# Softplus of the Mamba step in four VectorE instructions, with new orders of issue

## The reference

```python
xdbc = xi @ Wx
dt_in = xdbc[..., :DT_RANK]                       # 8 columns
dt = jax.nn.softplus(dt_in @ Wdt + bdt)           # 256 channels, bdt in -4 .. -2
def step(h, inp):                                 # over the 512 tokens
    dA = jnp.exp(dt_t[:, :, None] * A)
    h = dA * h + (dt_t * u_t)[:, :, None] * B_t[:, None, :]
    y = jnp.einsum('bds,bs->bd', h, C_t)
```

## Time and profile before

| | |
|---|---|
| median of 3 runs | 2081.15 us (2073.28 to 2085.22) |
| the profiled execution's own time | 2084.03 us |
| its span | 2081.9 us, 27272 instructions |
| busy | PE 1770.7 (85%), DVE 1582.0 (76%), ACT 1093.9 (53%), POOL 798.9 (38%) |
| mean granted TensorE clock | 0.919 |
| chain that ended last | PE 49%, DVE 18%, issue 14%, ACT 8%, POOL 5%, DMA 2% |
| ScalarE table loads | 196, 1283 ns each |

### The profile page before, as it was taken

One profiled execution on the slowest core, in us unless ns is written; L12 is line 12 of the kernel. 1 busy time (PEld: TensorE's weight loads), 2 busy tenths in 40 slices (PEclk: granted clock), 3 DMA queues, 4 the chain that ended last, 5 costly groups with the idle time before them and its releaser, 6 DMA issues.

```text
span 2081.9 us, 27272 instructions
## 1 busy us (share of the span) xinstructions
PE 1770.7 (85%) x8504; PEld 818.7 (39%) x8544; DVE 1582.0 (76%) x2148; ACT 1093.9 (53%) x1494; POOL 798.9 (38%) x632
## 2 busy tenths in 40 slices
PE   4543488989988999989998999989998999989888
PEld 1220133443343434443343434443444435434545
DVE  1888888779886898879986898869987899641404
ACT  2424376357734775357734676367734675334122
POOL 0345544244543454234543445235533446220101
PEclk9665698999999999999999999999999999999989
DMA  7889998458845786458745786558745786400000
GB/s 211 223 208 222 225 218 206 112 147 193 195 105 147 168 203 167 119 136 196 194 106 144 168 204 165 123 137 194 194 116 136 167 204 184 107 11 0 6 1 5
DMA packets 108200, 310.54 MB, mean 149 GB/s; under 512 B 16000, under 2 KB 32272, under 8 KB 108048
## 3 DMA queue, kind: packets, MB, share of 16 engines
q1 hardware_dynamic: 93840, 280.36, 56.1%
q10 hardware_dynamic: 14208, 28.32, 4.2%
HBM read 288.71 MB, written 19.92 MB: 148 GB/s over the span
## 4 chain that ended last, share of the span: by engine, by line
PE 49%; DVE 18%; issue 14%; ACT 8%; POOL 5%; DMA 2%; DVEq 1%; ACTq 0%; POOLq 0%
PE ps_pair L700 11%; PE ps_pair L856 8%; PE ps_pair L797 8%; DVE sb_hst L1278 6%; PE ps_pair L785 6%; PE ps_pair L650 4%; PE ps_pair L876 3%; POOL sb_hc L1540 3%; ACT sb_mix L1100 2%; PE ps_y L632 2%; DMA sb_ring<-spread_dram 2%; DVE ps_in L1270 2%; DVE sb_dd L1256 2%; DVE sb_dd L1252 2%; PE ps_pair L800 2%
## 5 line engine op out<-in xcount | busy, mean ns | idle before, releaser
L1540 POOL TENSOR_TENSOR sb_hc<-sb_hst,sb_crep 128x512 f32<-128x512 f32 x512 | 658.8, 1296 | 891.4 <-DVE sb_hst L1278 566.0
L1278 DVE TENSOR_TENSOR_SCAN sb_hst<-sb_ring,ps_in 128x512 f32<-128x512 f32 x512 | 621.4, 1214 | 74.6 <-POOL sb_hc L1540 50.6
L952 ACT ACTIVATE sb_ring<-sb_ring,sb_A 128x512 f32<-128x512 f32 x512 | 344.1, 712 | 163.3 <-DMA sb_ring<-spread_dram 105.3
L1270 DVE TENSOR_TENSOR ps_in<-sb_ring,ps_brow 128x512 f32<-128x512 f32 x512 | 354.6, 693 | 21.5 <-DMA sb_ring<-spread_dram 4.1
L856 PE MATMUL ps_pair<-sb_mix,sb_ew 128*128 128x512 f32 x512 | 270.6, 668 | 6.1 <-DVE sb_g L1357 3.3
L921 ACT ACT_TABLE_LOAD x196 | 251.5, 1283 | 14.3 <-DVE sb_xd L1318 5.6
L632 PE MATMUL ps_y<-sb_hc,sb_const 128*32 128x512 f32 x1024 | 153.1, 673 | 70.7 <-POOL sb_hc L1540 58.4
L797 PE MATMUL ps_pair<-sb_g,sb_h 128*128 128x512 f32 x320 | 161.4, 627 | 26.8 <-ACT sb_mix L1100 12.0
L785 PE MATMUL ps_pair<-sb_h,sb_g 128*128 128x512 f32 (+3 forms) x512 | 164.6, 453 | 5.1 <-DVE sb_nmax L1409 4.3
L856 PEld LDWEIGHTS ps_pair<-sb_mix,sb_ew 128*128 128x128 f32 x512 | 103.0, 212 | 154.9 <-issue 115.0
L876 PEld LDWEIGHTS ps_pair<-sb_ew,sb_eh 128*128 128x128 f32 x1024 | 120.0, 192 | 23.3 <-issue 22.5
(11 more groups left out here) (218 smaller groups left out, 2147.0 us busy)
## 6 DMA issues: line engine op xcount, KB each, us to landing
sb_ring<-spread_dram SPq DMA_DIRECT2D x512, 512.0 KB, 5.7
spread_dram<-sb_dd ACTq DMA_DIRECT2D x32, 512.0 KB, 2.9
sb_brep<-cut_dram ACTq DMA_DIRECT2D x16, 256.0 KB, 3.7
sb_crep<-cut_dram ACTq DMA_DIRECT2D x16, 256.0 KB, 4.0
sb_xtok<-in_L_attn_x_dram SPq DMA_DIRECT2D x8, 256.0 KB, 5.0
sb_ew<-in_L_ffn_w_dram SPq DMA_DIRECT2D x2, 1024.0 KB, 8.4
out_dram<-sb_yy ACTq DMA_DIRECT2D x8, 256.0 KB, 2.3
sb_h<-in_L_ffn_h_w_dram SPq DMA_DIRECT2D x1, 1024.0 KB, 7.3
```

Source lines behind the costliest of these rows:

```text
L952: act.activation(ring[:, n % RING, 0, :], ring[:, n % RING, 0, :], ACT.Exp, scale=A[d][:, g:g + 1]).then_inc(sem["dA"], 1)
L1270: dve.tensor_tensor(ps_in[n % 2][:], ring[:, n % RING, 1, :], ps_brow[:], ALU.mult).then_inc(sem["dbu"], 1)
L1278: dve.tensor_tensor_scan(hst[:, HST_SLOT[n], :], ring[:, n % RING, 0, :], ps_in[n % 2][:], 0.0, ALU.mult, ALU.add).then_inc(sem["scan"], 1)
L1540: pool.tensor_tensor(hc[:, n % 6, :], hst[:, HST_SLOT[n], :], crep[n // NU][:], ALU.mult).then_inc(sem["hc"], 1)
```

## The change

The bias becomes a row of the dt product: sb_wdt has 41 rows per direction (8 weights, 32 zeros, the bias), sb_xd a row of ones behind B and C. ScalarE's Identity becomes Square(t / sqrt(3) - 0.75 / sqrt(3)), to which 0.8125 is added, the same polynomial; GpSimd's product is gone; the mask is made by ScalarE as Relu(0.008 - t) in a tile of its own (sb_tsel), where a bit pattern other than zero counts as true. VectorE then has four instructions (and the memset of one column as before): series, masked copy, max(v, 0) plus logarithm out of PSUM in one, times u. The bank of a dtp product is released by dt, not by the early maximum. The first loads wait for GpSimd's memset of sb_wdt. A half takes two steps of the head stream where it took three, GpSimd has no head stream, and all order strings are written anew.

```diff
 def freed_head(name):
     if name[:3] == "dtp":
-        return "rpos", int(name[3]) + 1
+        return "dt", int(name[3]) + 1
 ...
 ORDER = dict(
     PE=(
-        "xxxxxxuxxxxrxruxrxrxruxrurxrhrurhhhrxhrhuhrrurxhhhxurruxhhxrrhurhhhxhxurhxxrhrhurhrrrrrrrrrrrrrrrurrrrxxhrrrrr"
+        "xxxxxxuxrxxruxrxhrurxhrurxuhxxrrhrrxhrrrurhhhuxrrrurxurhxxuxhrhxxrrxxhrrrurxrrrrrrrrrrrrhrhhuhrurhurrxrrrrrrru"
 ...
             with nc.allow_non_contiguous_dma(reason="per-channel vectors, once"):
+                sp.wait_ge(w_zero, 1)
 ...
-                rows = slice(64 * d, 64 * d + R)
+                rows = slice(64 * d, 64 * d + R + 2 * S + 1)
 ...
             def dt_step(row, hf, made):                      # ScalarE
-                act.wait_ge(sem["dt"], row("dt", hf))
+                act.wait_ge(sem["du"], row("du", hf))
                 act.wait_ge(sem["kept"], row("kept", 16 * hf))
-                act.activation(dd[:, 0, :], made()[:], ACT.Abs, bias=cols[d][:, 1, h:h + 1]
-                               ).then_inc(sem["absd"], 1)
+                act.activation(dd[:, 0, :], made()[:], ACT.Abs).then_inc(sem["absd"], 1)
 ...
-                act.activation(tser, texp[:], ACT.Identity, scale=1.0 / 3.0, bias=mhalf[:, 0:1]
+                act.activation(tser, texp[:], ACT.Square, scale=THIRD, bias=vertex[:, 0:1]
                                ).then_inc(sem["third"], 1)
+                act.activation(tsel[:], texp[:], ACT.Relu, scale=-1.0, bias=small[:, 0:1]).then_inc(sem["small"], 1)
                 act.activation(dd[:, 0, :], texp[:], ACT.Ln, bias=one[:, 0:1]).then_inc(sem["logd"], 1)
 ...
-            def dt_step(row, hf, k, made):                   # VectorE
-                if k == 0:
-                    dve.wait_ge(sem["absd"], row("absd", hf + 1))
-                    dve.tensor_scalar(tpos[:], made[:], cols[d][:, 1, h:h + 1], 0.0,
-                                      ALU.add, ALU.max).then_inc(sem["rpos"], 1)
-                elif k == 1:
-                    dve.wait_ge(sem["series"], row("series", hf + 1))
-                    link(1, dve.scalar_tensor_tensor(tser, tser, 1.0, texp[:], ALU.add, ALU.mult))
-                    dve.wait_ge(sem["logd"], row("logd", hf + 1))
-                    link(2, dve.tensor_scalar(tsel, texp[:], SMALL, None, ALU.is_le))
-                    dve.memset(tick[:], 0.0)
-                    link(3, dve.copy_predicated(dd[:, 0, :], tsel, tser))
-                    dve.tensor_tensor(dd[:, 0, :], dd[:, 0, :], tpos[:], ALU.add).then_inc(sem["dt"], 1)
+            def dt_step(row, hf, made):
+                dve.wait_ge(sem["third"], row("third", hf + 1))
+                dve.scalar_tensor_tensor(tser, tser, 0.8125, texp[:], ALU.add, ALU.mult).then_inc(sem["series"], 1)
+                dve.wait_ge(sem["series"], row("series", hf + 1))
+                dve.wait_ge(sem["small"], row("small", hf + 1))
+                dve.wait_ge(sem["logd"], row("logd", hf + 1))
+                dve.memset(tick[:], 0.0)
+                dve.copy_predicated(dd[:, 0, :], tsel[:].bitcast(U32), tser).then_inc(sem["log1p"], 1)
+                dve.wait_ge(sem["log1p"], row("log1p", hf + 1))
+                dve.scalar_tensor_tensor(dd[:, 0, :], made[:], 0.0, dd[:, 0, :], ALU.max, ALU.add).then_inc(sem["dt"], 1)
                 dve.wait_ge(sem["dt"], row("dt", hf + 1))
                 dve.tensor_tensor(dd[:, 1, :], dd[:, 0, :], u[d][:, h, :], ALU.mult).then_inc(sem["du"], 1)
 ...
-            def dt_step(row, hf):                            # GpSimd
-                pool.wait_ge(sem["third"], row("third", hf + 1))
-                pool.tensor_tensor(tser, tser, texp[:], ALU.mult).then_inc(sem["series"], 1)
```

101 lines of the change are left out of this document (44 added, 57 removed).

## The result

The changed kernel takes 2058.86 us in the median of four runs (2051.44 to 2060.53), the kernel before, run beside it, 2082.07. The ratio is 0.9888 with a 95% interval of 0.985 to 0.9927: 1.1% faster. The forecast was 2048 with a range of 2018 to 2092, so the time lies in the range and 11 us above the forecast. The sum behind the forecast did worse than that: its main term, 25 us from the five passes of the loop, came to 3.7.

The account below looks back on a forecast made before the run. TensorE, busy 92% of a pass, was taken to set the time, with VectorE's softplus making it wait. Six items sum to -5.0 us a pass; -37 in all from 2084, 2.9 to the median, 4 put back: 2048, range 2018 to 2092.

Parts of the forecast that it names:

- VectorE's saving: Softplus on VectorE: three instructions out, one in of 0.744 us; saves 2.05 us a half, 8.2 us a pass.
- Item 1: TensorE's pause before dtp3 goes, as VectorE starts half 2's series earlier; gain 3.66 + 3.4 = 7.1 us a pass.
- item 2: TensorE's pause before the query product goes, as half 0's softplus leaves xn's way; gain 3.40 + 3.3 = 6.7 us a pass.
- the prediction's own sign: TensorE's pauses before dtp3 and the query product: the forecast is wrong if they come back at other products.
- Item 3: x0 moves behind the last score, where TensorE had waited for the split (1.04 us); gain 1.9 us a pass.
- Item 4: dtp3's bank held until dt: second h2 product waits about 1 us, the norm's chain costs 1; loss 2 a pass.
- Item 5: One more unit (0.69 + 1.21 us) among the score maxima, where VectorE has no slack; loss 2 us a pass.
- Item 6: dtp1 between second and third block of exponentials: 3.3 us waiting plus a slow stretch of 3.4; loss 6.7 a pass.
- B: ScalarE takes VectorE's place: Relu and table loads, 5.2 us mid-pass, eat the gain; 2081, chance 0.18 with D.
- D: VectorE's saving is off the path and the pauses come back elsewhere; 2081, sharing B's chance of 0.18.
- C: Slower by the third block of exponentials alone, slipping behind VectorE's gate and reductions; 2092 at 8 us, chance 0.17.
- A: The order does better: no slow stretch behind dtp1, no cost for dtp3's bank; -10.4 us a pass, 2013, chance 0.12.

Follow-up runs that it names:

- Experiment 2: Changed kernel with ScalarE's spread DMA of half 2 issued later, behind the decay exponentials of units 26 to 29: 2046.2 us.
- experiment 9: Changed kernel with dtp3 behind the up product of expert 5 (up5) on TensorE: 2089.1 us.
- experiment 10: Changed kernel with ScalarE's spread DMAs of half 2 later, half 1 earlier, dtp3 behind up5, VectorE's gate of half 2 three units earlier: 2076.73 us.
- experiment 12: Changed kernel with ScalarE's spread DMAs of half 2 later, half 1 earlier, dtp3 behind up5, VectorE's eh of expert 5 before half 3's softplus: 2027.78 us.
- experiment 1: Kernel before with its order strings unchanged and only the new softplus arithmetic: 2071.07 us.
- experiment 3: Changed kernel with dtp1 and its softplus behind the last block of exponentials on TensorE, ScalarE and VectorE: 2049.38 us.
- experiment 4: Changed kernel with dtp1 and its softplus behind the last block of exponentials, and ScalarE's spread DMA of half 2 later: 2040.31 us.
- experiment 8: Changed kernel with ScalarE's Relu (the mask) done twice per half: 2081.26 us.
- experiment 7: Changed kernel with VectorE's masked copy of the softplus done twice per half: 2091.31 us.
- experiment 6: Changed kernel measured again, since the moved step issues nothing and every engine's instructions stayed the same: 2057.04 us.
- experiment 11: Changed kernel with spread DMA of half 2 later, dtp1 behind the last block, dtp3 behind up5, VectorE's gate of half 2 three units earlier: 2087.51 us.
- experiment 5: Changed kernel with ScalarE's spread DMA of half 1 issued earlier, behind unit 56's exponential: 2047.23 us.

## Why the prediction was right in the range and wrong in its main term

**VectorE's saving.** Forecast 2.05 us a half, measured 3.1, with busy time down by 95 us against 50 to 80. What I counted, three instructions out and one in, was right (2.11 by the measured 692 ns); the other 0.97 us are the series and the masked copy, which stayed and which I had left at their old price beside GpSimd. The Trainium skill, "SBUF — State Buffer", says under "SBUF: two separate sides" that VectorE and GpSimd take turns at a shared pair of ports when VectorE reads two inputs from SBUF and GpSimd reads there too, or when VectorE works in a mode that uses two ports. The trace agrees: L1252, with one input in PSUM, takes 690 to 693 ns in all 32, while L1245, with both in SBUF, takes 665 to 1400. The prediction put the rule too widely, that one input in SBUF is never slowed: the old mask (L1254) reads one, and it took 0.43 us in 11 cases and 1.37 to 1.38 in the other 21, all of these beside GpSimd.

**Item 1 and item 2, the two pauses.** Right in place and size for the two products. Both waits (3.66 and 3.40 us) and both slow stretches behind them are gone: the windows there have clocks of 1.00. But ScalarE still stood idle ahead of its spread DMA, 6.28 us and not none as I had said. The pause left TensorE and not ScalarE, and came back one Gelu later, ahead of up5, as 1.74 us (1.32 to 1.87 over the passes). Experiment 2 showed it. By the prediction's own sign, a pause that comes back at another product, item 1 is wrong to that extent. It had also misread the idle time as all waiting. Before the change it ran from 997.03 to 1002.39 us, and the spread DMA stands in its midst:

```profile
1000.57 0.35 ACTq L997 DMA_DIRECT2D spread_dram<-sb_dd  x1
```

So ScalarE waited 3.5 us for VectorE then, and it waits 3.5 us now; what lies behind, up to the next instruction, is the three DMA steps, 1.8 us then and 2.8 now.

**Item 3.** Right: nothing waits at x0, and the wait for the split is 0.26 us where it was 1.04.

**Item 4, dtp3's bank.** This step failed. I had about 1 us for the second h2 product and 1 for the norm's chain. The h2 product waits 2.19 us in every pass, and in three of five passes 1.6 more of slow clock stand behind it (0.86 in the windows above), so the bank costs 2.2 to 3.8 us; the norm's chain shows no wait over 0.2. With the 1.74 us of item 1 it is 4 to 5.6 and not 2. Experiments 9, 10 and 12 showed that it is the bank: with another bank that is freed later TensorE waits 5.5 to 5.7 us and the time rose by 30 us (experiment 9), with one freed early the wait was gone. In experiment 1 the same kind of wait came with the old order.

**Item 5.** From the first score to the last it is 23.7 us (572.09 to 595.8, in the loop's first pass) against 21.4 (1071.89 to 1093.3); I had 2. Right.

**Item 6, the third block.** Right to the place: block 2 starts 18.3 us after the split's end here (1088.30 after 1070.02) and 17.8 in the loop's first pass, where I had 17.9, with the slow stretch behind it (0.73). The waits are 0.55 + 1.60 + 1.86 + 1.45 = 5.5 us, where 1.21 and 1.19 stood before; the difference is 3.1 and I had 3.3. Experiments 3 and 4 showed that moving dtp1 away gives back only 2.5 us, since the gate is next.

**What was not in the sum.** At the jump back to the loop's start x3 comes 3.19 to 4.04 us after the mix, before the change 1.98 to 2.47, and outside the loop 1.55 to 1.65 in both. That is 1.5 us at each of the four jumps. The new order puts the spread DMA of half 1 at 1126.25, 7 us ahead of x3. Experiment 12 has it early and comes to 2.3 us; what the runs say of the cause stands at the end.

With 2 to 3.6 more for items 1 and 4 together and 1.2 a pass for the jumps, the forecast of -5.0 becomes -1.8 to -0.2; measured -0.75. Five passes gave 3.7 us and not 25.

**The rest of the program.** The last pass is right (6.9, forecast 6). The stretch up to the loop gave 12.5 us where I had 6: the first product of the second pass starts at 233.34 and before at 238.83, so 5.5 came from the first pass, which I had called held by DMA and given 1 us. I had read a DMA share of 0.89 as a bound, and it was none: the same stretch now has 0.96. With the arithmetic alone (experiment 1) x3 starts at 437.39, 2.6 us earlier and not 12.5, so most of it is the new order of the start; which part of that, no run here tells. It is the largest single gain of the change, and the prediction took it for 6 us, five of them by analogy with the loop.

**The rivals.** B and D had 2081 with the saving off the path. In the passes of the loop the gain was indeed nearly eaten, but by the banks and the jump. ScalarE's own time does count (experiment 8: 2.5 us for 2.8), though it still stood idle 6.28 us at the DMA. D's reason falls: experiment 7 prices 3.7 us of VectorE's time at 4.5. C did not come; the third block was as late as forecast and no later. A was excluded by the slow stretch.

The forecast of 2048 thus came within 11 us by luck: 21 us too much in the passes met 6.5 too little at the start, 2 in the last pass and the end, and 4 that I had put back for what might be late.

## What to carry to other kernels

When an instruction is merged with a later one, ask what the early one had freed. Here the early maximum had released a PSUM bank, and the merged one kept it until dt; in the loop that, with the slower jumps, took back most of what the shorter VectorE series and the new order gave. When TensorE waits for a bank, look at what stands ahead of the freeing instruction on its in-order engine before moving the product: the same move cost 30 us in one VectorE order and left no wait in the other (where two ScalarE edits stood beside it). And if a wait vanishes on one engine, check that the idle time of the engine that caused it vanished too, and how much of that idle time is waiting and how much is DMA steps.

## What the runs showed of the hardware

The jump back to the loop's start takes a time of its own, and it differs with what is around it. Measured from VectorE's mix to x3, less the same outside the loop:

| run | spread DMA issued ahead of x3 | extra at the four jumps |
|---|---|---|
| before | 16 us | 0.5, 0.9, 0.4, 0.6 |
| experiment 1 | 16 us | 0.3, 0.4, 0.6, 0.5 |
| changed kernel | 7 us | 2.2, 1.6, 2.2, 2.4 |
| experiment 2 | 7 to 9 us | 4.1, 2.2, 1.8, 1.9 |
| experiment 6 | 7 to 9 us | 2.1, 2.1, 2.4, 3.7 |
| experiment 7 | 7 us | 2.2, 2.2, 2.3, 2.6 |
| experiment 8 | 7 to 9 us | 2.7, 2.2, 3.6, 2.2 |
| experiment 9 | 7 us | 2.5, 2.0, 2.0, 2.3 |
| experiment 3 | 1.5 to 3.6 us | 1.3, 0.8, 2.9, 1.1 |
| experiment 4 | 1.5 to 3.5 us | 0.8, 2.6, 1.0, 0.9 |
| experiment 11 | 1.4 to 2.1 us | 1.4, 1.2, 1.2, 1.6 |
| experiment 5 | some 40 us | 2.3, 0.5, 1.9, 0.4 |
| experiment 10 | some 40 us | 2.4, 0.9, 0.8, 2.5 |
| experiment 12 | some 40 us | 0.5, 0.6, 0.9, 0.6 |

The DMA view of the changed kernel from 1129 to 1134 us, the stretch ahead of x3 (packets, MB, share of 16 engines):

```profile
q1 hardware_dynamic: 661, 0.79, 66.8%
q10 hardware_dynamic: 129, 0.46, 23.9%
q8 instruction: 2, 0.03, 2.7%
q14 instruction: 2, 0.02, 1.3%
```

Two queues of the kind "instruction" move packets while the data queues hold 91% of the engines; in the kernel before, from 1143 to 1147 us, one data queue held 74%. That the engines' code waits behind the data is my reading. The rows with 16 us and with 7 to 9 speak for it, all short and all long. The others speak against its simple form: in experiments 3, 4 and 11 the DMA is nearer still and most jumps are shorter, and in experiments 5, 10 and 12 it is far, and two, two and none of the four are long. It stays open.
